# Flamingo block on one core: the routing stage in front of the expert pages is rearranged

## What is computed

```
xf = layernorm(x)                                   # 8192 x 256
scores = sigmoid(xf @ gate_weight.T)                # 8 experts
choice = scores + bias
group_scores = sum of the 2 choices of each of 4 groups; keep the 2 best groups
topk_idx = the 2 best experts of the kept groups
topk_weight = scores at topk_idx, divided by their sum
y = sum over the two experts of weight * (silu(xf @ gate_proj[e].T) * (xf @ up_proj[e].T)) @ down_proj[e].T
x = x + tanh(g_ffn[1]) * y
```

## Time and profile before

| what | value |
|---|---|
| median of three runs | 1731.82 us (1730.54 to 1734.18) |
| the profiled execution's own time | 1729.68 us |
| its span, first to last instruction | 1727.9 us |
| mean granted clock of TensorE | 0.934 of 2.4 GHz |
| `expert_stage`, routing | 1261.6 to about 1410 us of the span |
| TensorE busy 1261 to 1286 / 1286 to 1313 / 1313 to 1339 / 1339 to 1366 | 18.6 / 18.7 / 23.5 / 22.4 us |
| VectorE busy in the same four stretches | 17.8 / 24.2 / 22.6 / 22.6 us |
| pages, 1410 to 1728: TensorE busy | 252.6 of 318 us |

### The profile page before, as it was taken

One profiled execution on the slowest core, in us unless ns is written; L12 is line 12 of the kernel. 1 busy time (PEld: TensorE's weight loads), 2 busy tenths in 40 slices (PEclk: granted clock), 3 DMA queues, 4 the chain that ended last, 5 costly groups with the idle time before them and its releaser, 6 DMA issues. The chain is left out here.

```text
span 1727.9 us, 46320 instructions
## 1 busy us (share of the span) xinstructions
PE 1340.8 (78%) x16924; PEld 976.5 (57%) x16924; DVE 1341.1 (78%) x2820; ACT 1191.0 (69%) x2029; POOL 942.5 (55%) x1132
## 2 busy tenths in 40 slices
PE   1699999756676776774999999999868628888886
PEld 0577777524444444443666766676657516666664
DVE  7799999757888888885789999999778825555553
ACT  1799999788877787762788888888741115555553
POOL 1466555427777777783334343434214657776775
PEclk9999999979999999996999999999985569999999
DMA  9400000090000000000000000000001222222220
GB/s 314 126 4 4 4 3 4 3 285 1 1 1 1 1 1 1 1 1 18 2 3 3 3 3 22 21 24 18 3 1 57 91 79 77 77 79 80 80 54 20
DMA packets 64218, 67.88 MB, mean 39 GB/s; under 512 B 14091, under 2 KB 59663, under 8 KB 64016
## 3 DMA queue, kind: packets, MB, share of 16 engines
q1 hardware_dynamic: 54208, 47.96, 9.4%
q0 software_dynamic: 7440, 17.06, 2.8%
q10 hardware_dynamic: 2368, 0.02, 0.1%
HBM read 35.14 MB, written 32.88 MB: 39 GB/s over the span
## 5 line engine op out<-in xcount | busy, mean ns | idle before, releaser
L775 ACT ACTIVATE a_exp<-a_score_t 128x1024 f32<-128x1024 f32 x256 | 263.5, 1029 | 37.0 <-PE a_score_t L566 36.1
L1160 POOL TENSOR_TENSOR b_hidden<-b_hidden,b_shifted 128x508 f32<-128x508 f32 x128 | 161.6, 1262 | 119.9 <-DVE b_hidden L1010 119.9
L840 POOL TENSOR_TENSOR a_split<-ctx,a_split 128x256 f16<-128x256 f32 x64 | 42.9, 670 | 271.1 <-ACT a_split L794 271.1
L1167 POOL TENSOR_TENSOR b_hidden<-b_hidden,b_scales 128x512 f32<-128x512 f32 x128 | 168.1, 1317 | 2.3 <-ACT b_scales L1142 2.3
L941 PE MATMUL b_hid<-b_x_turned,w1t 128*128 128x512 f16 x512 | 139.7, 398 | 26.4 <-DVE b_hidden L1010 23.1
L697 DVE TENSOR_REDUCE a_neg_max<-a_score 128x8 f16<-128x1024 f32 x128 | 156.0, 1219 | 1.8 <-PE a_score L551 1.2
L694 DVE TENSOR_REDUCE a_maxes<-a_score 128x8 f32<-128x1024 f32 x128 | 155.5, 1215 | 0.2
L1346 PE MATMUL e_bank<-e_wt,e_turned 128*128 x1092 | 150.1, 279 | 0.1
L1010 DVE SCALAR_TENSOR_TENSOR b_hidden<-b_hid,taps,b_hidden 128x508 f32<-128x508 f32 x128 | 94.8, 741 | 53.6 <-ACT b_shifted L1122 53.6
L806 ACT ACTIVATE a_k_turned<-a_turn 128x1024 f16<-128x1024 f16 x128 | 130.8, 1022 | 5.6 <-PE a_turn L601 5.6
L963 PE MATMUL b_peaks<-ident,b_hidden 128*128 128x128 f32 x512 | 85.3, 292 | 56.8 <-ACT b_hidden L1102 48.4
(11 more groups left out here) (250 smaller groups left out, 3962.4 us busy)
## 6 DMA issues: line engine op xcount, KB each, us to landing
e_rows<-blank SPq DMA_DIRECT2D x1, 12012.0 KB, 38.7
e_page<-e_rows SPq DMA_DIRECT2D x91, 132.0 KB, 2.1
x<-in_x SPq DMA_DIRECT2D x3, 2048.0 KB, 18.5
ctx<-in_ctx SPq DMA_DIRECT2D x1, 4096.0 KB, 26.9
a_q_turned<-a_neg_max_t SPq DMA_DIRECT2D x256, 2.0 KB
ctx<-in_ctx SPq DMA_DIRECT2D x1, 3072.0 KB, 16.4
a_exp<-in_L_ffn_w SPq DMA_DIRECT2D x2, 1024.0 KB, 9.2
x<-in_x SPq DMA_DIRECT2D x1, 1536.0 KB, 16.1
```

Of the source, the lines that this page charges most:

```text
L775: nc.scalar.activation(exp32[:, u % 2, 2 * p:2 * p + 2, :], score_t[:, :].rearrange("p (g n) -> p g n", g=2), ACT.Exp, scale=DH ** -0.5 / ...
L1160: nc.gpsimd.tensor_tensor(dst, dst, shifted[:, c % 2, :].rearrange("p (t k) -> p t k", k=P)[:, :, 0:P - 1], ALU.add).then_inc(conv_ok, 1)
L1167: nc.gpsimd.tensor_tensor(h, h, scales[:, (u - back) % 2, :], ALU.mult).then_inc(mult_ok, 1)
```

## The change

- The norms go from VectorE to ScalarE, as an activation with scale `rstd` and bias `-mean * rstd` (`shift`, one new operation on VectorE). In ScalarE's list `norm(q + 2)` stands ahead of `copy_pair(q)`.
- The experts' weights are no longer turned in the first chunk. Chunk j (1 to 3) has `make_hi(j - 1)` at its start on ScalarE, the high part's turn behind the logits of its second pair and the low part's behind those of its fifth; ScalarE copies both parts, behind its copies of the fourth and seventh pair. `make_low(j)` stands behind `weigh(j)` on VectorE.
- A class is found by the sum of 2^a + 2^b of the two experts, compared with 28 constants, instead of by a formula of them; the pair itself is made in `weigh`, which picks the two scores first and normalises the two alone.
- `new_pages` and `slots` read the counts in PSUM and keep `need` in the scan's first buffer; there are three operations fewer in `new_pages`.
- Of the 15 constants two go, and 36 memsets of one column each are added that wait for nothing.
- The row scatters have no bounds check.

```diff
-CONSTS = 15
+CONSTS = 13 + EXPERTS + CLASSES
@@ TensorE
                 def places(j):
                     pe.wait_ge(hot_ok, j + 1)
-                    reach(pe, index_ok, j)
+                    reach(pe, state_ok, j)
...
                 for q in range(last_pair):
-                    if q < 6:
-                        turn_expert(q // 2, q % 2)
                     logits_pair(q)
+                    if q >= pairs and q % pairs in (1, 4):
+                        turn_expert(q // pairs - 1, (1, 4).index(q % pairs))
@@ VectorE
                 def classify(j):
                     then(nc.vector.scalar_tensor_tensor(out=ranked[:], in0=rank8[:], scalar=float(TOP),
+                                                        in1=powers[:, None, :].broadcast_to([P, CT, EXPERTS]), op0=ALU.is_lt, op1=ALU.mult))
+                    then(nc.vector.tensor_reduce(key[:], ranked[:], AX.X, ALU.add))
+                    reach(dve, pos_ok, j)
+                    nc.vector.tensor_tensor(hot[:, 0:CT, :], key[:, :, None].broadcast_to([P, CT, CLASSES]),
+                                            classes[:, None, :].broadcast_to([P, CT, CLASSES]), ALU.is_equal).then_inc(hot_ok, 1)
...
                 def new_pages(j):
                     dve.wait_ge(pos_ok, j + 1)
-                    then(nc.vector.tensor_copy(count[:], place_ps[:, CT * CLASSES:(CT + 1) * CLASSES]))
-                    then(nc.vector.tensor_tensor(over[:], count[:], room[:], ALU.subtract))
-                    then(nc.vector.tensor_scalar(over[:], over[:], 0.0, 1.0 / P, ALU.max, ALU.mult))
-                    then(nc.vector.tensor_scalar(need[:], over[:], (P - 1) / (2.0 * P), MAGIC, ALU.add, ALU.add))
-                    then(nc.vector.tensor_scalar(need[:], need[:], MAGIC, None, ALU.subtract))
-                    then(nc.vector.tensor_copy(scan[:, 0, 16:], need[:]))
+                    then(nc.vector.scalar_tensor_tensor(out=over[:], in0=counted, scalar=(P - 1) / 2.0, in1=room[:], op0=ALU.add, op1=ALU.subtract))
+                    then(nc.vector.tensor_scalar(over[:], over[:], 1.0 / P, MAGIC, ALU.mult, ALU.add))
+                    then(nc.vector.tensor_scalar(need, over[:], MAGIC, None, ALU.subtract))
...
                 for j in range(CHUNKS):
                     choose_groups(j)
-                    norms(0)
                     choose_experts(j)
-                    norms(1)
                     classify(j)
-                    norms(2, 3)
                     weigh(j)
-                    norms(4, 5)
+                    if j + 1 < CHUNKS:
+                        make_low(j)
                     new_pages(j)
-                    norms(6)
                     slots(j)
-                    norms(7)
@@ ScalarE
+                def norm(q):
+                    reach(act, t_turn, q - NR + 1)
+                    for k in range(2):
+                        t = 2 * q + k
+                        last = nc.scalar.activation(normed[:, q % NR, k * D:(k + 1) * D], m.x[:, t, :], ACT.Identity,
+                                                    scale=m.rstd2[:, t:t + 1], bias=shift[:, t:t + 1])
+                    last.then_inc(norm_ok, 1)
...
+                act.wait_ge(shift_ok, 1)
+                norm(0)
+                norm(1)
+                for q in range(last_pair):
+                    j, k = q // pairs, q % pairs
+                    if j and k == 0:
+                        make_hi(j - 1)
+                    if q + 2 < last_pair:
+                        norm(q + 2)
+                    copy_pair(q)
+                    if j and k in (3, 6):
+                        copy_expert(j - 1, (3, 6).index(k))
+                    if k == pairs - 1:
+                        probabilities(j)
@@ GpSimd
+                at = 0
+                for a in range(EXPERTS):
+                    nc.gpsimd.memset(powers[:, a:a + 1], float(2 ** a)).then_inc(const_ok, 1)
+                    for b in range(a + 1, EXPERTS):
+                        nc.gpsimd.memset(classes[:, at:at + 1], float(2 ** a + 2 ** b)).then_inc(const_ok, 1)
+                        at += 1
...
                     for t in range(j * CT, (j + 1) * CT):
-                        nc.gpsimd.indirect_dma_start(rows_in, bass.IndirectOffsetOnAxis(ap=index[:, t:t + 1], axis=0), m.rows_sb[:, t, :], None,
-                                                     bounds_check=PAGES * P - 1, oob_is_err=False).then_inc(scattered, 16)
+                        nc.gpsimd.indirect_dma_start(rows_in, bass.IndirectOffsetOnAxis(ap=index[:, t:t + 1], axis=0), m.rows_sb[:, t, :], None).then_inc(scattered, 16)
```

More of the change, by code:

```diff
@@ L1219, in expert_stage @@
         turned32 = sb("turned32", [P, 2, 2, DC, P])
-        score, choice, weight, ranked = (sb(n, [P, CT, EXPERTS]) for n in ("score", "choice", "weight", "ranked"))
+        score, choice, ranked = (sb(n, [P, CT, EXPERTS]) for n in ("score", "choice", "ranked"))
         group, rank4, rank8 = sb("group", [P, CT, EGROUPS]), sb("rank4", [P, CT, EGROUPS]), sb("rank8", [P, CT, EXPERTS])
         ahead4, ahead8 = sb("ahead4", [P, CT * EGROUPS, EGROUPS - 1]), sb("ahead8", [P, CT * EXPERTS, EXPERTS - 1])
-        total, pair, half = sb("total", [P, CT]), sb("pair", [P, CT, TOP]), sb("half", [P, CT])
+        total, pair, key = sb("total", [P, CT]), sb("pair", [P, CT, TOP]), sb("key", [P, CT])
         of_pair = sb("of_pair", [P, CT, TOP, EXPERTS])
@@ L1227, in expert_stage @@
         slot, index = sb("slot", [P, CT]), sb("index", [P, TILES], U32)
-        end, room, fresh, over, need, step_to = (sb(n, [P, CLASSES]) for n in ("end", "room", "fresh", "over", "need", "step_to"))
-        scan = sb("scan", [P, 2, 16 + CLASSES])
+        end, room, fresh, over, step_to = (sb(n, [P, CLASSES]) for n in ("end", "room", "fresh", "over", "step_to"))
+        scan = sb("scan", [P, 3, 16 + CLASSES])
+        shift = sb("shift", [P, TILES])
         pages = sb("pages", [P, 1])
@@ L1393, in then @@
                     dve.wait_ge(chain, done[0])
[L1395 to L1401, removed]
                 def make_low(n):
@@ L1452, in weigh @@
                     here = extra[:, j * CT:(j + 1) * CT, :]
-                    then(nc.vector.scalar_tensor_tensor(out=weight[:], in0=rank8[:], scalar=float(TOP), in1=score[:], op0=ALU.is_lt, op1=ALU.mult))
-                    then(nc.vector.tensor_reduce(total[:], weight[:], AX.X, ALU.add))
+                    weights = here[:, :, WEIGHT - D:WEIGHT - D + TOP]
+                    then(nc.vector.scalar_tensor_tensor(out=ranked[:], in0=rank8[:], scalar=float(TOP),
+                                                        in1=experts[:, None, :].broadcast_to([P, CT, EXPERTS]), op0=ALU.is_lt, op1=ALU.mult))
@@ L1455, in weigh @@
+                    then(nc.vector.tensor_tensor(of_pair[:], of_pair[:], score[:, :, None, :].broadcast_to([P, CT, TOP, EXPERTS]), ALU.mult))
+                    then(nc.vector.tensor_reduce(weights, of_pair[:], AX.X, ALU.add))
+                    then(nc.vector.tensor_reduce(total[:], weights, AX.X, ALU.add))
                     then(nc.vector.tensor_scalar(total[:], total[:], 1e-20, WS, ALU.add, ALU.mult))
                     then(nc.vector.reciprocal(total[:], total[:]))
-                    then(nc.vector.tensor_tensor(weight[:], weight[:], total[:, :, None].broadcast_to([P, CT, EXPERTS]), ALU.mult))
@@ L1458, in weigh @@
[L1458 to L1461, removed]
+                    then(nc.vector.tensor_tensor(weights, weights, total[:, :, None].broadcast_to([P, CT, TOP]), ALU.mult))
@@ L1475, in new_pages @@
                     run = scan[:, 1, 16:]
-                    then(nc.vector.scalar_tensor_tensor(out=fresh[:], in0=run, scalar=pages[:, 0:1], in1=need[:], op0=ALU.add, op1=ALU.subtract))
-                    then(nc.vector.tensor_tensor(pages[:], pages[:], run[:, CLASSES - 1:CLASSES], ALU.add))
+                    then(nc.vector.scalar_tensor_tensor(out=fresh[:], in0=run, scalar=pages[:, 0:1], in1=need, op0=ALU.add, op1=ALU.subtract))
                     then(nc.vector.scalar_tensor_tensor(out=fresh[:], in0=fresh[:], scalar=float(P), in1=room[:], op0=ALU.mult, op1=ALU.subtract))
@@ L1479, in new_pages @@
                     then(nc.vector.tensor_tensor(step_to[:], end[:], fresh[:], ALU.subtract))
+                    then(nc.vector.tensor_tensor(pages[:], pages[:], run[:, CLASSES - 1:CLASSES], ALU.add))
                 def slots(j):
```

112 lines of the change are left out of this document (35 added, 77 removed).

## The result

The changed kernel takes 1721.88 us (median of 20 runs, 1717.9 to 1726.3); the kernel before, on the same chip beside it, 1728.66 us (20 runs, 1724.4 to 1734.5). The medians are 6.8 us apart. The ratio is 0.9951, interval 0.9940 to 0.9962: faster by 0.49%, which would be 8.5 us. The prediction's 1729.5 us was 2.3 us under the median it was made against; 1721.88 lies outside its range of 1723 to 1738. Part of that is the base (the kernel before was first given as 1731.82, from three runs), but the forecast itself was about no change, and the nearest rival, three rises of the clock, had a gain of 4.3 us where the two profiled executions differ by 5.70.

What follows compares the result with a forecast made beforehand. The stretch before the page loop was taken as bound by TensorE's last logits, paced by its clock, and the work up to the last scatter: +10.8 - 1.8 - 8.4 - 0.8 = -0.2 us, 1729.5 us, range 1723 to 1738.

Steps and rivals of the forecast that it cites:

- three rises of the clock: Rival: TensorE's clock rises in all three later chunks, GpSimd's third lot of scatters takes over as bound; 1725.4 us; chance 0.14.
- The start: TensorE's wait for constants: 36 memsets add 1.1 us, two dropped operations save 0.67; first token transposes at 1266.2.
- The first chunk: TensorE at the low clock throughout, without weight transposes; first sigmoid at 1286.8 us.
- The wait at a chunk's start: TensorE waits 3.65 us for ScalarE's copy, behind sigmoid, `make_hi` and norms, in each of chunks two to four.
- the rises: TensorE's clock going high around `places` in chunks two to four: two of three, 4.2 us back each.
- The case without a rise: Rival: clock never rises after the first idle time; later chunks 29.4 us each at low clock; 1737.9 us; chance 0.11.
- the window of 66 instructions: TensorE at 2.4 GHz: 5.5 pairs of tiles in 6.8 us, taken as 1.24 us a pair.
- The tail: VectorE in the last chunk, from the last sigmoid to `index`: 18.25 us instead of 20.06, `weigh`'s growth hidden behind `places`.
- The bounds check: GpSimd's last sixteen row scatters: dropping it saves 0.05 us each, -0.8 us.
- The rule of the Trainium skill: Rival: any sustained work raises TensorE's clock, first sigmoid at 1280, then four lots on GpSimd; 1710 us; chance 0.03.

Runs made afterwards that it cites:

- the small operations alone: The kernel before with only the changed `classify`, `weigh`, `new_pages`, `slots` and constants; norms, weights and bounds check as before: ratio 0.9976 to the kernel before.

## Why the prediction was wrong, point by point

- **The start** held: first transposes at 1265.92 (1266.2 forecast), the 36 memsets 0.03 us apart.
- **The first chunk** held: low clock throughout, sigmoid at 1286.80 (1286.8). The wait at a chunk's start is 3.59 us, from the sigmoid at 1286.80 to the logits at 1290.39 (3.65).
- **The step that failed is the rises**, "two of three" and "4.2 us" each, 8.4 us in all. There were three of three, nine of nine over three profiles, and they gave back 3.6, 6.2 and 6.0 us (29.4 less the intervals): 15.8, that is 7.4 us more than the forecast had. Against that stand 1.34 us for GpSimd's late last lot, which the sum did not have, and 0.6 us that the scatters gave less; so -0.2 becomes the measured -5.70 within 0.1 us. The count went by one rise in three stretches of one trace of the kernel before, a base too small. The size assumed that the high clock begins behind `places` and lasts 6.8 us, though in the same trace it had been high for 20 us of the first chunk (1269.5 to 1289.5). In the second of these chunks it began ahead of `places`, which then took 1.85 us (1324.43 to 1326.28) instead of 3.6, and twice it lasted 10.2 us. My reason for a chance over a half, the weight transposes close by, is not borne out: two versions without them there (the small operations alone, the weights back) also show a rise in each of the three chunks. Nor is it the norms' move: two versions with the norms on VectorE (the small operations alone, the norms back) have one or more in each chunk. What made them rarer in the two traces of the kernel before, three in six chunks, stays open.
- **The case without a rise** was sized rightly: the version with `places` cut has chunks of 28.3 to 29.4 us, with one short rise.
- **Two small slips:** the window of 66 instructions that gave 1.24 us a pair begins with the end of `places`; from pair to pair it is 1.28 us (transposes at 1301.60, 1302.88 and 1304.16). And the chances for "faster" add up to 0.35, not 0.36. Neither moves the sum by more than some tenths.
- **The rival of three rises** describes what happened: GpSimd's third lot takes over as the bound of the last (1379.49 against 1381.5 forecast), 1725.4 us for the profiled execution against 1723.98. It had 0.14. That the total comes so near is in part GpSimd's doing: the last `index` came 3.2 us before this rival's (1377.4 against 1380.6), but the last lot only 2.0 us, and the scatters gave 0.6 us less.
- **The tail** held: 18.11 us (18.25 forecast), `weigh` hidden with 0.32 us to spare.
- **The bounds check** held at the low end: 0.011 us a scatter, not 0.05.
- **Missed:** `make_low` was costed at nothing, hidden behind `places` on VectorE. It holds up GpSimd: two of the scatters under it took 2.84 and 2.37 us instead of 0.96, 3.3 us in all. Here that lay ahead of GpSimd's waits for the next `index`; with the idle matmuls, where GpSimd is the bound, it counts.
- **The rule of the Trainium skill (TensorE: Matmul & The Clock Gate, Part 1)** that sustained activity releases the throttle was put at 0.03. From 1265 to 1286 the granted clock was 0.50 with TensorE busy for 20.1 of the 21 us, so here too the row decides against the rule.

## What to carry to other kernels

Before costing a change of the order of TensorE's work, ask at which of its two clocks each stretch runs and what stands in it: the same matmuls in another order were 11 us apart here, and a few idle matmuls in the waits gave as much again as the change. Two engines near their limit hide each other's gains (idle matmuls in the kernel before 3.5 us, where they did not keep the clock throughout; the change alone 8.5; both 21), so try both before one is put aside. And do not take a chance from one trace: profile the kernel before twice.

## What the runs showed of the hardware that was not expected

Beside `make_low`, a VectorE operation with two operands in SBUF, the issue of an indirect DMA on GpSimd took up to three times as long. Timelines of both engines in the changed kernel:

```profile
1322.68 0.96 POOL L1656 DMA_INDIRECT e_rows<-x,e_index  x1 [0.31 <-issue]
1323.66 2.29 DVE L1396 SCALAR_TENSOR_TENSOR ctx<-ctx 128x2048 f16<-128x2048 f32 x1
1323.94 2.84 POOL L1656 DMA_INDIRECT e_rows<-x,e_index  x1 [0.30 <-issue]
```

The scatter that starts while `make_low` runs takes 2.84 us instead of 0.96, until 0.8 us after its end. So did the one beside the next `make_low` (2.37 us), two in the version with idle matmuls (2.84 and 1.89) and two with the norms back (2.87 each). The other way round, beside GpSimd's 128x2048 operations in the version with the split moved there, VectorE waited:

```profile
1262.65 16.37 POOL L1658 TENSOR_SCALAR ctx<-ctx 128x2048 f16<-128x2048 f32 x3
1268.17 11.27 DVE L1404 SCALAR_TENSOR_TENSOR ctx<-ctx 128x2048 f16<-128x2048 f32 x2 [9.14 <-POOL ctx L1658]
```

The Trainium skill (SBUF — State Buffer, "Who interferes with whom") has this: an instruction of VectorE with two SBUF inputs contends with one of GpSimd that reads SBUF, and the order of issue decides which of them is blocked. The trace agrees for GpSimd's arithmetic, with 11.27 us for two operations that take 2.29 us each when alone. Of descriptor generation the section reports that VectorE's `tensor_tensor` did not stall it in a probe; here the issue was stretched to 2.84 us beside a SCALAR_TENSOR_TENSOR, so for that the rows decide.

The high clock was kept for 33.9 us with the idle matmuls (two of 256 columns a pair, twelve at the chunk's start), where pairs alone lost it after 6.8 us with TensorE busy for 6.5 of them. It is no sure means: with the weights in the first chunk the clock fell at 1281, in the kernel before at 1287, and even in the version itself it was low from 1298.5 to 1302.
